# A decoder layer on one core: gate and query products in three fp32r products, with the low part of x taken on VectorE and both parts added on GpSimd

## The reference

```
x = x + retention(layernorm(x))          # A: 8 heads of 32
x = x + attention(layernorm(x), ctx)     # B: 16 heads of 16, causal
x = x + ffn(layernorm(x))                # C: 8 experts, 256 -> 1024 -> 256, gelu

# retention (A), xh = x by heads:
q, k, v = xh @ Wq, xh @ Wk, xh @ Wv
ret = (q k^T * decay) v,  normalised over each head, * gn_w + gn_b
gated = x @ W1
return (gated * sigmoid(gated) + ret) @ W2
```

## Time and profile before

| | |
|---|---|
| three runs | 371.53 us median (370.04 to 372.04) |
| the profiled execution | 369.38 us, its span 367.6 us |
| TensorE busy | 338.3 us, 92% of the span |
| VectorE, ScalarE, GpSimd busy | 254.6, 238.9, 163.5 us |
| transfers | 26.97 MB, 73 GB/s over the span |
| TensorE's granted clock | full in all 40 slices |

### The profile page before, as it was taken

One profiled execution on the slowest core, in us unless ns is written; L12 is line 12 of the kernel. 1 busy time (PEld: TensorE's weight loads), 2 busy tenths in 40 slices (PEclk: granted clock), 3 DMA queues, 4 the chain that ended last, 5 costly groups with the idle time before them and its releaser, 6 DMA issues.

```text
span 367.6 us, 8998 instructions
## 1 busy us (share of the span) xinstructions
PE 338.3 (92%) x3283; PEld 280.1 (76%) x3299; DVE 254.6 (69%) x555; ACT 238.9 (65%) x586; POOL 163.5 (44%) x148
## 2 busy tenths in 40 slices
PE   7878679999999999999999999999999998989697
PEld 3657457987789877987789867987789866858596
DVE  5674786677766976677775976678765966482974
ACT  4552663776756866677847766677848764787551
POOL 4237150364615366363625457362634550445340
PEclk9999999999999999999999999999999999999999
DMA  5940102022031400413023400404014300013300
GB/s 151 307 172 1 31 2 107 37 62 85 1 112 78 144 0 17 171 33 110 0 66 120 143 0 14 169 7 137 0 47 141 116 6 10 30 16 116 116 29 30
DMA packets 22314, 26.97 MB, mean 73 GB/s; under 512 B 2896, under 2 KB 20112, under 8 KB 22288
## 3 DMA queue, kind: packets, MB, share of 16 engines
q1 hardware_dynamic: 21472, 26.52, 22.3%
q10 hardware_dynamic: 816, 0.10, 0.2%
HBM read 24.51 MB, written 2.10 MB: 72 GB/s over the span
## 4 chain that ended last, share of the span: by engine, by line
PE 77%; DVE 9%; issue 7%; ACT 4%; POOL 1%; DMA 1%; ACTq 0%; DVEq 0%; POOLq 0%
PE c L1208 22%; PE a L1208 16%; PE b L1208 14%; PE b1k L1344 7%; PE b1k L1208 6%; PE b2k L1208 4%; DVE negmax L912 2%; PE c L1371 2%; ACT prob L596 1%; ACT probT L558 1%; PE a L1223 1%; DVE scD L893 1%; PE b2k L1223 1%; DMA wk_c<-in_L_attn_Wk 1%; PE a L1301 1%
## 5 line engine op out<-in xcount | busy, mean ns | idle before, releaser
L460 POOL TENSOR_TENSOR w_lo<-w_in,w_hi 128x512 fp32r<-128x512 f32 x32 | 40.8, 1305 | 30.4 <-ACT w_hi L558 26.3
L596 ACT ACTIVATE prob<-b,negmax 128x128 f32<-128x128 f32 x124 | 36.1, 398 | 25.4 <-DVE negmax L912 25.4
L1344 PE MATMUL b1k<-ident,prob 128*128 128x128 f32 x256 | 40.0, 279 | 9.3 <-ACT probT L558 4.5
L466 POOL TENSOR_TENSOR w_lo<-w_in,w_hi 128x512 fp32r<-128x512 f32 x28 | 35.5, 1287 | 28.6 <-ACT w_hi L558 26.8
L453 POOL TENSOR_TENSOR rstA<-varA,minus_half 128x16 f32<-128x16 f32 x8 | 23.4, 2927 | 49.2 <-DVE varA L1047 49.2
L1344 PEld LDWEIGHTS b1k<-ident,prob 128*128 128x128 f32 x256 | 28.1, 140 | 17.3 <-ACT prob L596 7.2
L558 ACT ACTIVATE w_hi<-w_in 128x512 fp32r<-128x512 f32 x64 | 39.1, 653 | 2.6 <-PE b L1208 2.6
L1208 PE MATMUL c<-xTC_hi,w_hi 128*128 128x256 f32 x108 | 31.8, 294 | 0.8 <-DVE xTC_lo L862 0.8
L919 DVE COPY probT<-b1k 128x512 f32<-128x512 f32 x32 | 22.0, 687 | 13.1 <-PE b1k L1344 13.0
L1208 PE MATMUL c<-w_hi,h_hi 128*128 128x256 f32 x96 | 30.8, 321 | 0.1
L1208 PE MATMUL c<-xTC_lo,w_hi 128*128 128x256 f32 x108 | 30.5, 282 | 0.0
(11 more groups left out here) (301 smaller groups left out, 1110.4 us busy)
## 6 DMA issues: line engine op xcount, KB each, us to landing
w_in<-in_L_ffn_w SPq DMA_DIRECT2D x16, 1024.0 KB, 5.6
x_in<-in_x SPq DMA_DIRECT2D x8, 256.0 KB, 2.8
c_in<-in_ctx SPq DMA_DIRECT2D x8, 256.0 KB, 2.9
out<-x2b SPq DMA_DIRECT2D x7, 256.0 KB, 2.2
b_cur<-in_L_ffn_b SPq DMA_DIRECT2D x8, 128.0 KB, 3.0
W_sb<-in_L_attn_W SPq DMA_DIRECT2D x2, 256.0 KB, 4.2
decay_sb<-in_decay SPq DMA_DIRECT2D x1, 512.0 KB, 3.8
h_in<-in_L_xattn_Wk SPq DMA_DIRECT2D x1, 256.0 KB, 4.3
```

Of the source, the lines that this page charges most:

```text
L460: pool.tensor_tensor(w1_lo[:, :, part], w1_in[:, :, part], w1_hi[:, :, part].bitcast(F32), ALU.subtract).then_inc(s_w1lo, 1)
L466: pool.tensor_tensor(w2_lo[:, part, :], w2_in[:, part, :], w2_hi[:, part, :].bitcast(F32), ALU.subtract).then_inc(s_w2lo, 1)
L596: ins = nc.scalar.activation(prob[:, u % PR, g, :], score_banks[u][:, g * P:(g + 1) * P], ACT.Exp, bias=negmax[:, u, g:g + 1], scale=-1.0)
L1344: ins = nc.tensor.transpose(b1k[:, g * P:(g + 1) * P], prob[:, u % PR, g, :], ident[:, :])
```

## The change

ScalarE's copy of the transposed x goes, from step 1 on, to an fp32r tile `xTA_hi` in place of `xTA`. VectorE takes the bank less `xTA_hi` into `xTA_lo` (`split_x`), behind the copy of `probT` and ahead of the statistics of x1; in body 0 it stands behind the statistics. GpSimd adds both parts into `xTA` (`whole_x`), behind rsB, for the value products and the scores, which stay fp32; the value products wait for it. The gate and the query products of steps 1 to 7 become three fp32r products each, and gate piece 0 waits for the low part in place of ScalarE's copy. At the start GpSimd makes both parts of `W1` and of `qk_bd`. Step 0 keeps its fp32 products.

```diff
+        W1_hi = sb("W1_hi", [P, C, D], F32R)        # likewise W1_lo, qk_hi, qk_lo, xTA_hi, xTA_lo
...
 # GpSimd, body
+                def whole_x(step):
+                    pool.wait_ge(s_xTAlo, step)
+                    pool.tensor_tensor(xTA[:, :, :], xTA_hi[:, :, :].bitcast(F32), xTA_lo[:, :, :].bitcast(F32),
+                                       ALU.add).then_inc(s_xTA, 1)
...
                 if do_a:
                     rsqrt(a, rsB[:, :], mvB[:, :, 1], s_lnB, 4, s_rsB, NB)
+                if nextA:
+                    whole_x(a + 1)
...
 # GpSimd, before the bodies
+            pool.wait_ge(s_wvbd, RJ)
+            pool.wait_ge(s_W1, 16)
+            pool.wait_ge(s_qkc, 1)
+            wait_apart(pool)
+            for w, hi in ((W1_sb, W1_hi), (qk_bd, qk_hi)):
+                pool.tensor_scalar(hi[:, :, :], w[:, :, :], 1.0, None, ALU.mult).then_inc(s_Whi, 1)
+            pool.wait_ge(s_Whi, 2)
+            for w, hi, lo in ((W1_sb, W1_hi, W1_lo), (qk_bd, qk_hi, qk_lo)):
+                pool.tensor_tensor(lo[:, :, :], w[:, :, :], hi[:, :, :].bitcast(F32), ALU.subtract).then_inc(s_Wlo, 1)
...
 # ScalarE
             def transposed_x(step):
                 act.wait_ge(s_TA, step + 1)
-                copy(xTA[:, :, :], a0[:, :].rearrange("p (c t) -> p c t", c=C), s_xTA)
+                if later(step):
+                    copy(xTA_hi[:, :, :], a0[:, :].rearrange("p (c t) -> p c t", c=C), s_xTAhi)
+                else:
+                    copy(xTA[:, :, :], a0[:, :].rearrange("p (c t) -> p c t", c=C), s_xTA)
...
 # VectorE
+            def split_x(step):
+                dve.wait_ge(s_xTAhi, step)
+                nc.vector.tensor_tensor(xTA_lo[:, :, :], a0[:, :].rearrange("p (c t) -> p c t", c=C),
+                                        xTA_hi[:, :, :].bitcast(F32), ALU.subtract).then_inc(s_xTAlo, 1)
...
                 if do_b:
                     divide(0)
                     probT_odd(7)
+                    split_x(a + 1)
                 dve.wait_ge(s_x1, a + 1)
                 statistics(a, x1, statB, mvB, s_lnB)
+                if not do_b:
+                    split_x(a + 1)
                 if do_b:
                     divide(1)
...
 # TensorE
                 def ret_values(bank):
+                    pe.wait_ge(s_xTA, a + 1)
...
                 def ret_queries():
                     for k in range(C):
-                        ins = mm(a1[:, k * T:(k + 1) * T], qk_bd[:, k, :], xTA[:, k, :])
+                        out = a1[:, k * T:(k + 1) * T]
+                        if later(a):
+                            ins = mm_split(out, (qk_hi[:, k, :], qk_lo[:, k, :]), (xTA_hi[:, k, :], xTA_lo[:, k, :]))
+                        else:
+                            ins = mm(out, qk_bd[:, k, :], xTA[:, k, :])
                     ins.then_inc(s_qA, 1)
...
             def gate(step, piece):
                 m, k = piece // C, piece % C
-                if piece == 0:
-                    pe.wait_ge(s_xTA, step + 1)
-                ins = mm(a0[:, m * T:(m + 1) * T], W1_sb[:, k, m * P:(m + 1) * P], xTA[:, k, :],
-                         start=(k == 0), stop=(k == C - 1))
+                cols = slice(m * P, (m + 1) * P)
+                if not later(step):
+                    pe.wait_ge(s_xTA, 1)
+                    weights, x_parts = (W1_sb,), (xTA,)
+                else:
+                    weights, x_parts = (W1_hi, W1_lo), (xTA_hi, xTA_lo)
+                    if piece == 0:
+                        pe.wait_ge(s_Wlo, 2)
+                        pe.wait_ge(s_xTAlo, step)
+                ins = mm_split(a0[:, m * T:(m + 1) * T], [w[:, k, cols] for w in weights], [t[:, k, :] for t in x_parts],
+                               start=(k == 0), stop=(k == C - 1))
```

More of the change, by code:

```diff
@@ L89, in decoder_kernel @@
         W1_sb = sb("W1_sb", [P, C, D])
+        W1_hi = sb("W1_hi", [P, C, D], F32R)
+        W1_lo = sb("W1_lo", [P, C, D], F32R)
+        qk_hi = sb("qk_hi", [P, C, P], F32R)
+        qk_lo = sb("qk_lo", [P, C, P], F32R)
         W2_sb = sb("W2_sb", [P, C, D])
@@ L117, in decoder_kernel @@
         xTA = sb("xTA", [P, C, T])
+        xTA_hi = sb("xTA_hi", [P, C, T], F32R)
+        xTA_lo = sb("xTA_lo", [P, C, T], F32R)
         qA = sb("qA", [P, C, T])
@@ L239, in decoder_kernel @@
         s_xTA = signal("s_xTA")
+        s_xTAhi = signal("s_xTAhi")
+        s_xTAlo = signal("s_xTAlo")
+        s_Whi = signal("s_Whi")
+        s_Wlo = signal("s_Wlo")
         s_qA = signal("s_qA")
```

## The result

The changed kernel takes 372.75 us (median of 7, 372.32 to 374.28) against 371.53 before; the ratio is 1.0064, with a 95% interval of 1.0038 to 1.0089: slower, where 370.6 was forecast. Both intervals lie above one.

The account below looks back on a forecast made before the run. TensorE, busy 40.84 of 41.80 us per step, was the bound. Queries and gate piece 3 -1.0, gate piece 0 -0.1, late division +0.1, step 0 +0.05: -0.95 us, from 371.53 to 370.6; range 368.6 to 372.6.

Parts of the forecast that it names:

- GpSimd's sum of both parts: On GpSimd behind rsB: 1.28 us, done 3.8 us before the value products need it; cost 0.
- The clock in body 0: Rival, 8%: TensorE idle 2.8 us in step 0 drops the clock; kernel ends 1 to 5 us later, 373.5.
- The base: Profiled execution 369.38 us, to become 368.4; the same difference from the three-run median 371.53 gives 370.6.
- the forecast of -0.95: Whole kernel: sum of all gains and costs, -0.95 us, to 370.6; chance 60%.
- Query products and gate piece 3: Behind attention's output product: TensorE through 0.25 us sooner, 0.17 reaching the feed-forward products; 1.0 us in six steps.
- Gate pieces 1 and 2: Ahead of TensorE's 0.35 us wait for att: they save 0.17 us, the wait grows by it; gain 0.
- Gate piece 0: Between the transposes of the context and of pvT: gain 0.1 us in all, bounds 0 and 0.6.
- the bound that I had set aside: First fp32r record after fp32 work: taken as 0; bound 0.09 for each group, 1.9 us in 21 groups.
- The split on VectorE: Ahead of the second division: 0.61 us, hidden in idle time five times of six, late once; cost 0.1 us.
- TensorE's busy time: Check in the profile: smaller by about 0.5 us a step, the step shorter by only 0.1 to 0.2.

Follow-up runs that it names:

- e5: Kernel before the change plus, behind rsB in bodies 0 to 6, a GpSimd addition that nobody reads; ratio 1.0040 to the kernel before.
- e3: Changed kernel with only GpSimd's sum moved: ahead of rsB, in body 0 behind the wait for xnB; ratio 0.9999 to the kernel before.
- e4: Changed kernel with split, sum and fp32r products only from step 2 on and the sum ahead of rsB; ratio 0.9971 to the kernel before.
- e1: Changed kernel with 12 zero products filling TensorE's idle stretch in body 0; ratio 1.0022 to the kernel before.
- e6: Kernel before the change with TensorE made to wait for rsB in body 0, so it stands idle there; ratio 1.0075 to the kernel before.
- e7: Changed kernel with the sum moved as in e3 and 12 zero products in TensorE's idle stretch of body 0; ratio 0.9973 to the kernel before.
- e8: Kernel of e4 with eight zero products on TensorE in body 1; ratio 0.9936 to the kernel before.
- e13: Kernel before the change with zero products in body 1 (six and two) and the last body (nine); 369.39 us, ratio 0.9954.
- the second measurement: The changed kernel measured again, nothing altered; 372.38 us, ratio 1.0027 to the kernel before.
- e10: Kernel of e4 without the low products of the query products and gate piece 3 in steps 2 to 7; ratio 0.9981 to the kernel before.
- e9: Kernel of e4 without the low products of gate pieces 1 and 2 in steps 2 to 7; ratio 0.9982 to the kernel before.
- e14: Changed kernel, sum not moved, with zero products in body 0 (twelve), body 1 (six and two) and the last body (nine); 370.46 us, ratio 0.9984.
- e12: Kernel of e8 with nine more zero products in the last body; 368.62 us, ratio 0.9924 to the kernel before.

## Why the prediction was wrong, step by step

- **The step that failed: "GpSimd's sum of both parts ... cost 0".** I looked for who needs its result, found 3.8 us to spare, and did not ask what runs beside it. It holds the second instruction of `xnB`: 1.0 us in body 0 (e5, e3), and 0.15 a step later, a little more than the 0.11 that the query products gain (e4). My bounds for it had no upper end at all but "if the cover went".
- **The clock in body 0** was the rival with 8%. The mechanism was right, place and cause (e1, e6); its price was sized at 1 to 5 us and is 0.6 (e1) or 0.8 (e7 against e3) in the mean, each uncertain by 0.7, and 0.9 in the profile. It is likelier than not: all four profiles with that idle stretch have it (the changed kernel twice, e3, e6). I took a clock that stood through 2.00 us idle in one execution as evidence; e8 fell at that wait.
- **The base.** The forecast added a difference to the median as if that were the profiled kernel. The profile was at full clock throughout; the median holds falls in body 1 and in the last body, which cost 1.6 us in the mean (e13). No profile of the kernel before shows them; the places are those of the kernels made from it, and of e13's zero products. The spread of the three runs was not noise about one value. So how far the median lay beyond the range (372.75 against 372.6; the second measurement's 372.38 lies within) is the draw of the clock. The sign is not: at full clock, too, the forecast of -0.95 met +1.07.
- **Query products and gate piece 3:** right in mechanism. TensorE is through them 0.23 sooner (forecast 0.25); 0.11 of it reaches the feed-forward products (forecast 0.17, in six steps 1.0 us; measured 0.55 in five steps of e4, which makes 0.66 in six). More cannot come: e10 took 4.2 us of work away for nothing.
- **Gate pieces 1 and 2:** forecast 0, measured 0 (e9). Gate piece 0 gained nothing either: it takes 0.46 us (146.44 to 146.90), for the first fp32r product behind fp32 work costs about 0.09 (the next one starts 0.21 behind it, not 0.117), the bound that I had set aside.
- **The split on VectorE:** forecast hidden, and it is: the reciprocal is still released by the transposes of `pvT`, with 0.17 us idle left of 0.46 to 0.77. Its place in body 0 is what makes TensorE idle.
- **TensorE's busy time** of a step fell by 0.1 us and not by 0.5: matmul records overlap, so this column could not show it.

## What to carry to other kernels

When an instruction goes to an idle engine, ask what the other engines run in that very window, and which port or memory they share with it, not only who waits for its result. Look in the trace for instructions of one form whose longest time is far above the median, as `h_hi` with 1.53 us against 0.42, and at what runs beside them. Before a forecast from one profile, see whether that execution is a typical one: times in two or three clusters, or a mean granted clock that differs between executions, mean that a median and a profile belong to different cases. Cheap filler products in TensorE's thin stretches were worth 1.6 us here, more than the whole change in either direction, and cost nothing that shows at full clock (369.39 against 369.42).

## What the runs showed of the hardware that I had not expected

- A two-input GpSimd instruction of 1.3 us beside two short VectorE instructions that work in SBUF alone: the first ran in its usual 0.4 us, the second took 1.38 (0.98 longer). `cTB_lo`, which reads PSUM, was not slowed, and neither were the statistics of x1, which read SBUF and write little (0.74 us for the two at 184.28 of the kernel before, beside GpSimd's addition from 183.82 to 185.10).
- The granted clock differs from execution to execution: with the same program, the kernel before had mean clocks of 1.00, 0.995, 0.991 and 0.986, and times of 369.4, 370.2, 371.7 and 372.3 us. The places are stretches with waits of 1 to 2 us between little work; with zero products there, all executions kept it (12 of e13, 12 of e14, 6 of e12).
- Whether the two slow stretches of body 0 and body 1 influence each other stays open: no run filled only body 1 of the unrepaired kernel.
